# A language-model tower on one core: places of their own for the steps of groups 0, 1, 14, 15 and of the second half's groups 0, 1

## The chip, the cores and the metric

The kernel is one program on one core of a Trainium2 chip. The metric is the device time of one execution in microseconds (us). The kernel before was timed three times: 1875.1, 1875.68 and 1881.88 us, with a median of 1875.68 us. The profile comes from one further execution.

## What is computed

The input is 32 rows of 256 tokens. The reference, cut to what matters:

```python
h = tok_ref(x, ...)                       # embed, 2 layers, head: (32, 256, 256)
#   per layer: LN, q/k/v, causal convolution of k and v by 8 filters, gates,
#   gated linear attention (prefix sums), unit norm, wo, residual,
#   LN, gelu MLP 128-512-128, residual; at the end LN and head 128-256
h = h + attn_ref(_layernorm(h), W_q, W_k, W_v, W_o)   # linear attention, 16 heads of 64, not causal
h = h + ffn_ref(_layernorm(h), w_gate, w_up, w_down)  # silu(gate) * up, 256-768-256
return h
```

## The kernel before

The 32 batch rows are taken two at a time, so there are 16 groups of 512 tokens. The **tower** (function `token_tower`) runs every group through embedding, two layers and the head and stores 512 KB for it in `h_rows`. Its buffers exist four times (streams, group g uses stream g modulo 4). The **second half** (`attention_and_mlp`) loads these rows group by group on two streams, forms the linear attention and the gated MLP, and sends the result. Products of the large matrices are made of three fp32r matmuls (high by high, high by low, low by high), so nearly every input is split by ScalarE (the `high` steps) and VectorE (the `low` steps).

**The order of the work** is written out in tables. A step is a piece of a group's work on one engine: for example `turn` (four transposes on TensorE, L873), `high` (ScalarE, L764) and `low` (VectorE, L619) after it, `av` (TensorE, L972), `chain` (twelve small VectorE instructions ending at L706, a reciprocal square root by Newton steps), `unit` (TensorE, L1000), `mask` (VectorE, L679), `gated` (VectorE, L648 to L659), `q_out` (ScalarE, L773 and L775), `vT_out` (ScalarE, L788), `f1` (TensorE, L820 to L822), `f2` (L1028). In the second half there are `b_load` (a 512 KB load issued by SyncE, L1230), `b_stats` (VectorE, L1275), `rows_high` (GpSimd), `rows_low` (VectorE, L1302), `gram`, `t1`, `keys`, `r`, `m`, `attn` (TensorE), `b_turn` (TensorE, L1440), `b_gate`, `b_up`, `down` (TensorE).

`PLACES_A` and `PLACES_B` hold one place per step for the tower and the second half, `STARTS_A` and `STARTS_B` one start per group; `PREPARE` and `START_UP` hold the preparation of the weights. All steps are sorted by place plus start:

```python
steps = [(at + start, (step, g % STREAMS, l, j, g // STREAMS))
         for g, start in enumerate(STARTS_A) for step, l, j, at in PLACES_A]
...
steps.sort(key=lambda step: step[0])
order = [step for at, step in steps]
```

Each engine then walks this one list and issues the steps that are its own (L1549 to L1579), so that the list fixes the program order of every engine, SyncE's DMA issues included. It fixes the rotation of the PSUM banks too (`uses.add` along the list). Semaphores carry all dependences, so a step whose input is late holds up everything behind it on its engine.

The regions of the four streams are used again by the second half: its V and K weights lie in stream 0's, its rows of group 0 in stream 1's (`b_load` waits for the stores of tower groups 12 and 13), W_q's halves in stream 2's (after group 14's store), its rows of group 1 in stream 3's (after group 15's store). `m_high` waits for group 15's store, and `silu` for all four. `first(s, l, t)` (L462) marks the steps that also wait for the loads and preparations of the start.

Of the kernel before, what the change touches and what calls it, by code (L numbers as in the profile page):

```python
# [35 lines left out]
PLACES_A = [("embed", 0, 0, 832), ("stats", 0, 0, 904), ("pow", 0, 0, 975), ("shift", 0, 0, 944), ("xn", 0, 0, 980),  # L36
            ("turn", 0, 0, 952), ("high", 0, 0, 981), ("low", 0, 0, 974), ("bias", 0, 0, 1928), ("q", 0, 0, 1408),
            ("q_out", 0, 0, 1610), ("kv", 0, 0, 958), ("kv_out", 0, 0, 976), ("kv", 0, 1, 967),
            ("kv_out", 0, 1, 978), ("conv", 0, 0, 974), ("conv_out", 0, 0, 1374), ("conv", 0, 1, 977),
            ("conv_out", 0, 1, 1407), ("turn_v", 0, 0, 1411), ("vT_out", 0, 0, 1610), ("gate", 0, 0, 1650),  # L40
            ("gate_mul", 0, 0, 1791), ("gated", 0, 0, 1838), ("state", 0, 0, 1825), ("state_low", 0, 0, 1893),
            ("floor", 0, 0, 1915), ("qk", 0, 0, 1630), ("mask", 0, 0, 1731), ("qk", 0, 1, 1755),
            ("mask", 0, 1, 1854), ("av", 0, 0, 1815), ("av", 0, 1, 1839), ("av", 0, 2, 1856), ("av", 0, 3, 1877),
            ("apply", 0, 0, 1899), ("norm", 0, 0, 1920), ("sum", 0, 0, 1923), ("chain", 0, 0, 1959),
            ("unit", 0, 0, 1953), ("unit_out", 0, 0, 1974), ("wo", 0, 0, 1959), ("wo_out", 0, 0, 1977),
            ("stats", 1, 0, 1977), ("pow", 1, 0, 2283), ("shift", 1, 0, 1985), ("xn", 1, 0, 2074),
            ("turn", 1, 0, 1982), ("high", 1, 0, 2577), ("low", 1, 0, 2214), ("bias", 1, 0, 2724),
# [3 lines left out]
            ("pow", 2, 0, 2948), ("shift", 2, 0, 2921), ("xn", 2, 0, 2976), ("turn", 2, 0, 2935),  # L51
            ("high", 2, 0, 2981), ("low", 2, 0, 2966), ("bias", 2, 0, 3790), ("q", 1, 0, 2951),
            ("q_out", 1, 0, 2985), ("kv", 1, 0, 2943), ("kv_out", 1, 0, 2971), ("kv", 1, 1, 2946),
            ("kv_out", 1, 1, 2975), ("conv", 1, 0, 2958), ("conv_out", 1, 0, 2986), ("conv", 1, 1, 2960),
            ("conv_out", 1, 1, 2988), ("turn_v", 1, 0, 2967), ("vT_out", 1, 0, 2992), ("gate", 1, 0, 2973),
            ("gate_mul", 1, 0, 2984), ("gated", 1, 0, 2988), ("state", 1, 0, 2984), ("state_low", 1, 0, 2989),
            ("floor", 1, 0, 3579), ("qk", 1, 0, 2975), ("mask", 1, 0, 2984), ("qk", 1, 1, 2982),
            ("mask", 1, 1, 2988), ("av", 1, 0, 2983), ("av", 1, 1, 2985), ("av", 1, 2, 2986), ("av", 1, 3, 2989),
            ("apply", 1, 0, 2991), ("norm", 1, 0, 3599), ("sum", 1, 0, 2998), ("chain", 1, 0, 3282),
            ("unit", 1, 0, 3519), ("unit_out", 1, 0, 3640), ("wo", 1, 0, 3644), ("wo_out", 1, 0, 3791),  # L60
            ("stats", 3, 0, 3797), ("pow", 3, 0, 3942), ("shift", 3, 0, 3845), ("xn", 3, 0, 3823),
            ("turn", 3, 0, 3837), ("high", 3, 0, 3838), ("low", 3, 0, 3883), ("bias", 3, 0, 3947),
# [3 lines left out]
            ("pow", 4, 0, 3999), ("shift", 4, 0, 3979), ("xn", 4, 0, 3995), ("turn", 4, 0, 3981),  # L66
            ("high", 4, 0, 3999), ("low", 4, 0, 3995), ("head", 0, 0, 3994), ("head_out", 0, 0, 3995),
            ("head", 0, 1, 3995), ("head_out", 0, 1, 3996), ("idx", 0, 0, 2611), ("gather", 0, 0, 3031),
            ("gather", 0, 1, 3362), ("gather", 0, 2, 3429), ("gather", 0, 3, 3936), ("store", 0, 0, 3985)]
# [1 line left out]
PLACES_B = [("b_load", 0, 0, 102), ("b_stats", 0, 0, 667), ("b_pow", 0, 0, 838), ("b_xn", 0, 0, 859),
            ("b_turn", 0, 0, 1140), ("b_high", 0, 0, 1170), ("b_low", 0, 0, 1170), ("b_turn", 0, 1, 1159),
            ("b_high", 0, 1, 1224), ("b_low", 0, 1, 1182), ("rows_high", 0, 0, 991), ("rows_low", 0, 0, 906),
            ("gram", 0, 0, 930), ("gram_high", 0, 0, 905), ("gram_low", 0, 0, 930), ("gram", 1, 0, 962),
            ("gram_high", 1, 0, 1003), ("gram_low", 1, 0, 999), ("t1", 0, 0, 975), ("t1_even", 0, 0, 1055),
            ("t1_odd", 0, 0, 994), ("t1", 0, 1, 984), ("t1_even", 0, 1, 1075), ("t1_odd", 0, 1, 999),
            ("keys", 0, 0, 1025), ("keys_out", 0, 0, 1113), ("keys", 0, 1, 1075), ("keys_out", 0, 1, 1125),
            ("r", 0, 0, 1076), ("r_high", 0, 0, 1126), ("r_low", 0, 0, 1104), ("r", 0, 1, 1089),
            ("r_high", 0, 1, 1141), ("r_low", 0, 1, 1123), ("m", 0, 0, 1124), ("m", 0, 1, 1125), ("m", 0, 2, 1126),
            ("m_high", 0, 0, 1169), ("m_low", 0, 0, 1169), ("attn", 0, 0, 1181), ("attn_out", 0, 0, 1189),  # L80
            ("t1", 1, 0, 1000), ("t1_even", 1, 0, 1114), ("t1_odd", 1, 0, 1057), ("t1", 1, 1, 1112),
            ("t1_even", 1, 1, 1169), ("t1_odd", 1, 1, 1168), ("keys", 1, 0, 1142), ("keys_out", 1, 0, 1172),
            ("keys", 1, 1, 1145), ("keys_out", 1, 1, 1202), ("r", 1, 0, 1152), ("r_high", 1, 0, 1220),
            ("r_low", 1, 0, 1172), ("r", 1, 1, 1156), ("r_high", 1, 1, 1221), ("r_low", 1, 1, 1177),
            ("m", 1, 0, 1174), ("m", 1, 1, 1175), ("m", 1, 2, 1176), ("m_high", 1, 0, 1231), ("m_low", 1, 0, 1188),
            ("attn", 1, 0, 1182), ("attn_out", 1, 0, 1197), ("b_stats", 1, 0, 1197), ("b_pow", 1, 0, 1205),
            ("b_xn", 1, 0, 1219), ("b_turn", 1, 0, 1225), ("b_high", 1, 0, 1777), ("b_low", 1, 0, 1227),
            ("b_turn", 1, 1, 1230), ("b_high", 1, 1, 1859), ("b_low", 1, 1, 1231), ("b_gate", 0, 0, 1558),
            ("b_up", 0, 0, 1781), ("silu", 0, 0, 1900), ("hid", 0, 0, 1869), ("hid_high", 0, 0, 1979),
            ("hid_low", 0, 0, 1423), ("b_gate", 1, 0, 1778), ("b_up", 1, 0, 1834), ("silu", 1, 0, 1995),  # L90
            ("hid", 1, 0, 2074), ("hid_high", 1, 0, 2156), ("hid_low", 1, 0, 2326), ("b_gate", 2, 0, 1794),
            ("b_up", 2, 0, 1865), ("silu", 2, 0, 2003), ("hid", 2, 0, 2114), ("hid_high", 2, 0, 2493),
            ("hid_low", 2, 0, 2387), ("b_gate", 3, 0, 1913), ("b_up", 3, 0, 1961), ("silu", 3, 0, 2036),
            ("hid", 3, 0, 2220), ("hid_high", 3, 0, 2494), ("hid_low", 3, 0, 2423), ("b_gate", 4, 0, 1946),
            ("b_up", 4, 0, 2453), ("silu", 4, 0, 2117), ("hid", 4, 0, 2462), ("hid_high", 4, 0, 2496),
            ("hid_low", 4, 0, 2496), ("b_gate", 5, 0, 1970), ("b_up", 5, 0, 2467), ("silu", 5, 0, 2260),
            ("hid", 5, 0, 2468), ("hid_high", 5, 0, 2497), ("hid_low", 5, 0, 2499), ("down", 0, 0, 2422),
            ("down", 1, 0, 2445), ("down", 2, 0, 2467), ("down", 3, 0, 2471), ("down", 4, 0, 2495),
            ("down", 5, 0, 2499), ("add", 0, 0, 2497), ("add", 1, 0, 2498), ("send", 0, 0, 2183)]
# [1541 lines left out]
```

## Time and profile before

| | |
|---|---|
| median of 3 runs | 1875.68 us (1875.1 to 1881.88) |
| profiled execution | 1885.79 us, of which the span is 1883.7 us |
| TensorE matmuls busy | 1806.8 us (96% of the span) |
| VectorE busy | 1099.6 us (58%) |
| ScalarE, GpSimd busy | 726.2 us (39%), 424.4 us (23%) |
| granted TensorE clock, mean | 0.983 |

The tower takes about the first 850 us, the second half the rest; they overlap for some tens of microseconds. "Idle before" is the time that an engine stood still before an instruction, with what released it. A granted clock of 1.00 is 2.4 GHz, one of 0.50 is 1.2 GHz.

### The profile page before, as it was taken

To read this page: it belongs to the slowest core of one execution; us is meant where nothing else is said; L and a number is where in the kernel's file an instruction comes from. 1 tells how busy PE (TensorE), PEld (TensorE's weight loads), DVE (VectorE), ACT (ScalarE), POOL (GpSimd) and SP (SyncE) were. 2 spreads that over 40 slices of the span, in tenths; PEclk is the share of its full clock that TensorE was granted. 3 is DMA by queue.
4 is the path that set the end of the run, shared out by engine and by line. 5 is a ranking of instruction groups with operands and counts; after the bars stand their busy time and mean duration, and the time that the engine had idled before them with its cause. 6 is when DMAs were issued, how large, how long until landed. Compare 5 with 4: busy or idle time off the path is not lost.

```text
span 1883.7 us, 41798 instructions
## 1 busy us (share of the span) xinstructions
PE 1806.8 (96%) x17146; PEld 1583.0 (84%) x17146; DVE 1099.6 (58%) x2955; ACT 726.2 (39%) x1508; POOL 424.4 (23%) x391
## 2 busy tenths in 40 slices
PE   5899999999999999868999999999999999999998
PEld 4788888888888888657888888988888888888887
DVE  3688888888888887555444445444444444444443
ACT  2455555555555555423323232233233322323232
POOL 4233333333333322110122102210211121122102
PEclk9899999999999999878999999999999999999999
DMA  3000000000000001012000000000000000000000
GB/s 97 8 7 18 19 18 19 19 18 18 19 18 18 28 13 69 12 45 74 1 23 23 11 14 23 24 1 23 23 24 2 23 23 24 2 23 23 1 23 23
DMA packets 29355, 42.39 MB, mean 23 GB/s; under 512 B 6000, under 2 KB 22768, under 8 KB 29168
## 3 DMA queue, kind: packets, MB, share of 16 engines
q1 hardware_dynamic: 26160, 35.07, 5.7%
q0 software_dynamic: 2048, 4.20, 0.9%
q8 instruction: 138, 2.26, 0.5%
q10 hardware_dynamic: 960, 0.46, 0.1%
q14 instruction: 49, 0.40, 0.1%
HBM read 22.93 MB, written 16.78 MB: 21 GB/s over the span
## 4 chain that ended last, share of the span: by engine, by line
PE 80%; DVE 11%; issue 4%; DMA 2%; POOL 1%; ACT 1%; SPq 0%; DVEq 0%; POOLq 0%; ACTq 0%
PE ps L1426 14%; PE ps L1427 13%; PE ps L1428 13%; PE ps L1028 5%; PE ps L1476 3%; PE ps L972 3%; PE ps L1492 3%; PE ps L956 3%; PE ps L905 2%; PE ps L820 2%; DMA h<-h_rows 2%; PE ps L822 2%; PE ps L821 2%; PE ps L873 2%; PE ps L1440 2%
## 5 line engine op out<-in xcount | busy, mean ns | idle before, releaser
L1265 POOL TENSOR_TENSOR hids_low<-hid,hids_high 128x512 fp32r<-128x512 f32 x96 | 125.6, 1309 | 773.9 <-ACT hids_high L1412 773.9
L521 POOL TENSOR_TENSOR rstd<-var,minus_half 128x4 f32<-128x4 f32 x80 | 81.7, 1021 | 453.6 <-DVE var L608 453.6
L679 DVE TENSOR_TENSOR att<-ps,causal 128x512 f32<-128x512 f32 x256 | 158.8, 684 | 18.4 <-PE ps L956 17.1
L759 ACT ACTIVATE xn<-x,shift,rstd 128x128 f32<-128x128 f32 x320 | 131.3, 486 | 90.6 <-DVE shift L613 90.6
L1426 PE MATMUL ps<-r_high,wq_high 128*128 128x256 f32 x512 | 144.9, 283 | 0.6 <-issue 0.6
L1428 PE MATMUL ps<-r_high,wq_low 128*128 128x256 f32 x512 | 144.9, 283 | 0.0
L1427 PE MATMUL ps<-r_low,wq_high 128*128 128x256 f32 x512 | 144.9, 283 | 0.0
L1028 PE MATMUL ps<-w_f,wide 128*128 128x128 f32 x1024 | 127.1, 278 | 0.0
L1412 ACT ACTIVATE hids_high<-hid 128x512 fp32r<-128x512 f32 x96 | 60.4, 629 | 169.6 <-PE ps L1428 124.7
L1328 DVE TENSOR_TENSOR m_low<-ps,m_high 128x512 fp32r<-128x512 f32 x32 | 22.1, 691 | 176.8 <-ACT m_high L1398 176.8
L1028 PEld LDWEIGHTS ps<-w_f,wide 128*128 128x128 f32 x1024 | 119.4, 192 | 5.2 <-issue 5.0
L1322 DVE TENSOR_TENSOR r_low<-ps,r_high 128x512 fp32r<-128x512 f32 x128 | 79.5, 684 | 60.6 <-ACT r_high L1390 60.6
L1426 PE MATMUL ps<-wd_high,hids_high 128*128 128x256 f32 x384 | 111.4, 290 | 0.7 <-POOL hids_low L1265 0.7
L1406 ACT ACTIVATE silu<-ps 128x512 f32<-128x512 f32 x96 | 55.5, 594 | 141.2 <-PE ps L1428 106.6
L815 ACT ACTIVATE wide<-ps,b_f 128x512 f32<-128x512 f32 x128 | 83.1, 697 | 68.6 <-PE ps L822 68.5
L1314 DVE COPY t<-ps 128x512 f32<-128x512 f32 x64 | 44.3, 692 | 111.1 <-PE ps L1428 62.8
L1428 PE MATMUL ps<-wd_high,hids_low 128*128 128x256 f32 x384 | 108.7, 283 | 0.0
L1427 PE MATMUL ps<-wd_low,hids_high 128*128 128x256 f32 x384 | 108.5, 283 | 0.0
L1341 DVE TENSOR_TENSOR hid<-silu,ps 128x512 f32<-128x512 f32 x96 | 65.0, 683 | 66.4 <-PE ps L1428 54.1
L1426 PE MATMUL ps<-wv_high,gram_high 128*128 128x512 f32 x256 | 103.3, 404 | 0.0
L1398 ACT ACTIVATE m_high<-ps 128x512 fp32r<-128x512 f32 x32 | 19.1, 597 | 211.9 <-PE ps L1428 198.9
L1427 PE MATMUL ps<-wv_low,gram_high 128*128 128x512 f32 x256 | 99.8, 390 | 0.0
(350 smaller groups left out, 5042.2 us busy)
## 6 DMA issues: line engine op xcount, KB each, us to landing
h_rows<-h_out SPq DMA_DIRECT2D x16, 512.0 KB, 2.7
h<-h_rows SPq DMA_DIRECT2D x16, 512.0 KB, 3.9
out<-bxn SPq DMA_DIRECT2D x32, 256.0 KB, 2.3
emb<-in_embed,idx POOLq DMA_INDIRECT x64, 2.6
taps<-in_filters SPq DMA_DIRECT2D x1, 1024.0 KB, 5.7
stage<-in_W_vT SPq DMA_DIRECT2D x2, 512.0 KB, 5.7
wk<-in_W_kT SPq DMA_DIRECT2D x1, 1024.0 KB, 5.0
wo<-in_W_oT SPq DMA_DIRECT2D x1, 1024.0 KB, 9.4
```

Source lines behind the costliest of these rows:

```text
L521: pool.tensor_tensor(rstd[s][:], var[s][:], minus_half[:], ALU.pow)\
L679: dve.tensor_tensor(masked[:, :, PAIR * g:PAIR * g + PAIR, :], bank("qk", s, l, j, g, t)[:].rearrange("p (n r t) -> p n r t", n=2, r=PAIR) ...
L759: act.activation(xn[s][:, j, :], x[s][:, j, :], ACT.Identity, bias=shift[s][:, j:j + 1], scale=rstd[s][:, j:j + 1]).then_inc(xn_made[s].se ...
L815: act.activation(gl[s][:, j, :], bank("f1", s, l, j, t)[:], ACT.Gelu_apprx_tanh, bias=b_f1[:, l, j:j + 1]).then_inc(gl_made[s].sem, 1)
L1028: ins = pe.matmul(out[:, D * j:D * j + D], gl[s][:, f, P * j:P * j + P], w_f2[l][:, f, :], start=(f == 0 and j == 0), stop=(f == FC - 1), ...
L1265: pool.tensor_tensor(hids[1][:, halves, :], hid[:, half, :], hids[0][:, halves, :].bitcast(F32), ALU.subtract).then_inc(hid_low[s].sem, 1)
L1322: dve.tensor_tensor(low, bank("r", s, b, k, t)[:], high.bitcast(F32), ALU.subtract)\
L1341: dve.tensor_tensor(hid[:, uses.place["hid", s, b, t], :], silu[:, uses.place["silu", s, b, t], :], bank("b_up", s, b, t)[:], ALU.mult).th ...
L1412: act.activation(hids[0][:, uses.place["hids", s, b, t], :], hid[:, uses.place["hid", s, b, t], :], ACT.Copy).then_inc(hid_high[s].sem, 1)
L1426: pe.matmul(out, lhsT[0], rhs[0], start=start, stop=False, **kw)
L1427: pe.matmul(out, lhsT[0], rhs[1], start=False, stop=False, **kw)
L1428: return pe.matmul(out, lhsT[1], rhs[0], start=False, stop=stop, **kw)
```

## The change

No instruction that computes is added or removed. Four edits:

1. All places and starts of the common tables are multiplied by ten, which leaves their order as it was.
2. `MOVED_A` gives steps of tower groups 0, 1, 14 and 15 places of their own, `MOVED_B` steps of the second half's groups 0 and 1.
3. `PREPARE` and `START_UP` have new places. Steps of equal place from `START_UP` now come ahead of the tower's.
4. `first` holds for the first turn of all four streams, not of stream 0 alone, so the waits for loads and preparations are issued for groups 1, 2 and 3 too.

```diff
-STARTS_A = [547, 1549, 2550, 3551, 4553, 5555, 6557, 7559, 8560, 9562, 10563, 11565, 12567, 13569, 14570, 15572]
+STARTS_A = [5470, 15490, 25500, 35510, 45530, 55550, 65570, 75590, 85600, 95620, 105630, 115650, 125670, 135690,
+            145700, 155720]
+MOVED_A = [(0, "stats", 0, 0, -76025), (0, "shift", 0, 0, -76005), (0, "xn", 0, 0, 13137), (0, "turn", 0, 0, -45339),
...
+           (0, "kv_out", 0, 1, -75070), (0, "turn_v", 0, 0, 14315), (0, "vT_out", 0, 0, 15282),
...
+           (1, "shift", 0, 0, -85089), (1, "xn", 0, 0, 5589), (1, "turn", 0, 0, 8871), (1, "high", 0, 0, 5590),
...
+           (15, "turn", 3, 0, 29891), (15, "high", 3, 0, 37621), (15, "low", 3, 0, 36528), (15, "bias", 3, 0, 39502),
...
+MOVED_B = [(0, "b_load", 0, 0, -7399), (0, "b_stats", 0, 0, -108), (0, "b_pow", 0, 0, 984), (0, "b_xn", 0, 0, 796),
...
+           (0, "rows_high", 0, 0, 8680), (0, "rows_low", 0, 0, 5152), (0, "gram", 0, 0, 10),
...
+           (1, "b_load", 0, 0, -1393), (1, "b_stats", 0, 0, -5523), (1, "b_pow", 0, 0, -758),
...
+           (1, "rows_high", 0, 0, -459), (1, "rows_low", 0, 0, -5068), (1, "gram", 0, 0, -2327),
...
-    steps = [(at + start, (step, g % STREAMS, l, j, g // STREAMS))
+    moved = {(g, step, l, j): at for g, step, l, j, at in MOVED_A}
+    steps = [(moved.get((g, step, l, j), at) + start, (step, g % STREAMS, l, j, g // STREAMS))
              for g, start in enumerate(STARTS_A) for step, l, j, at in PLACES_A]
...
-    steps += [(at, (step, n, 0, 0, 0)) for step, n, at in START_UP]
+    steps[:0] = [(at, (step, n, 0, 0, 0)) for step, n, at in START_UP]
 
     def first(s, l, t):
-        return s == l == t == 0
+        return l == t == 0
...
-        steps += [(at + start, (step, g % B_STREAMS, b, n, g // B_STREAMS))
+        moved = {(g, step, b, n): at for g, step, b, n, at in MOVED_B}
+        steps += [(moved.get((g, step, b, n), at) + start, (step, g % B_STREAMS, b, n, g // B_STREAMS))
                   for g, start in enumerate(STARTS_B) for step, b, n, at in PLACES_B]
```

Sorting the two sets of tables by hand gives what changes for each engine. Of TensorE's 1652 steps the order differs in 270, all of them among the first 182 and among numbers 758 to 1028. Orders that matter below, of the kernel after:

| where | before | after |
|---|---|---|
| start, ScalarE | `q_out`, `vT_out` of group 0 | `vT_out`, `q_out` |
| start, VectorE | group 0: `mask`, `gate_mul`, `gated`, `mask` | `gate_mul`, `gated`, `mask`, `mask` |
| start, TensorE | group 0: `sum`, `unit`; group 1: `turn`; then `wo`, `kv`, `kv`, `conv`; `q` later | group 1 `turn`, `sum`, `f1_bias`, group 1 `kv`, `q`, then `unit`, `kv`, `wo`, `conv` |
| start, GpSimd | gathers of groups 1 and 2, then `embed` of group 1 | gathers of group 1, its `embed` and `pow`, then gathers of 2 and 3 |
| end of tower, TensorE | ..., `av` 0 and later steps of 15, both `head` of 14, `sum` 15, `unit` 15, `wo` 15, `turn` 15, three `f1` 15, `gram` of the second half's group 0 | `sum` 15, `unit` 15, `wo` 15, `gram`, `head` 14, `turn` 15, `head` 14, four `f1` 15 |
| end of tower, SyncE | store 14, then `b_load` 0 | store 13, `b_load` 0, then store 14 |
| end of tower, SyncE | store 15, `w_load` 4, 5, `b_load` 1, `w_load` 6 | `w_load` 4, 5, store 15, `w_load` 6, `b_load` 1 |
| end of tower, VectorE | group 15's `unit_out`, `b_stats` 0, `wo_out` | `b_stats` 0 ahead of 14's `f2_out` and 15's `gate_mul`; `unit_out`, `rows_low` 0, `wo_out` |
| second half, TensorE | `attn` 0, `attn` 0, `b_turn` 0, `b_turn` 0, `b_gate` 0 ... then `gram` of group 1 | a `gram` of group 1 amid `m` 0; `attn`, `attn`, `gram`, `t1`, `t1` of group 1, then `b_turn`, `b_turn`, `keys`, `keys`, `t1` of 1, `b_gate` 0 |

## Rows read from the trace of the kernel before

**Rows 1.** The page: span and busy time of TensorE.

```profile
span 1883.7 us, 41798 instructions
...
PE 1806.8 (96%) x17146; PEld 1583.0 (84%) x17146; DVE 1099.6 (58%) x2955; ACT 726.2 (39%) x1508; POOL 424.4 (23%) x391
```

**Rows 2.** Windows: length, busy time (and instructions) of each engine, clock, DMA share, GB/s.

```profile
0.00:47.00 47.00, 27.42 (x221) 21.98 (x221) 18.54 (x66) 11.27 (x26) 19.85 (x26) 0.93 0.38 98
47.00:94.00 47.00, 38.43 (x347) 33.40 (x348) 28.44 (x88) 19.94 (x43) 12.14 (x12) 0.82 0.03 8
...
376.00:470.00 94.00, 93.49 (x1055) 82.00 (x1053) 77.69 (x250) 50.81 (x115) 30.98 (x30) 1.00 0.06 18
...
752.00:800.00 48.00, 39.94 (x348) 33.06 (x349) 28.21 (x81) 21.12 (x45) 9.06 (x8) 0.89 0.03 12
800.00:848.00 48.00, 33.87 (x236) 28.46 (x237) 27.00 (x74) 13.28 (x25) 5.32 (x5) 0.79 0.14 44
848.00:896.00 48.00, 40.47 (x389) 34.94 (x388) 25.72 (x54) 17.43 (x30) 3.02 (x3) 0.89 0.22 72
```

**Rows 3.** Timeline of TensorE, the start: start, length, instruction, [idle before, releaser].

```profile
49.29 1.11 PE L1000 MATMUL ps<-ident,sq 128*128 128x128 f32 x4 [3.12 <-DVE sq L706]
...
57.08 3.27 PE L905 MATMUL ps<-wide,taps 128*128 128x128 f32 x16 [1.86 <-DVE wide L627]
...
83.92 0.58 PE L820 MATMUL ps<-w_kv1h,xT0h 128*128 128x256 f32 x1 [2.67 <-DVE xT0l L619]
```

**Rows 4.** Timeline of ScalarE and VectorE in the start, group 0's first layer.

```profile
29.02 1.45 ACT L773 ACTIVATE wide<-ps,b_q_part,parity 128x512 f32<-128x512 f32 x2 [0.22 <-PE ps L822]
...
30.72 0.60 ACT L788 ACTIVATE vT<-ps 128x512 f32<-128x512 f32 x1
...
32.62 2.48 DVE L679 TENSOR_TENSOR att<-ps,causal 128x512 f32<-128x512 f32 x4 [7.99 <-PE ps L956]
```

**Rows 5.** Timeline of TensorE, the end of the tower.

```profile
758.23 1.08 PE L972 MATMUL ps<-att,gk 128*32 128x128 f32 x16 [2.63 <-DVE gk L659]
...
780.90 0.50 PE L820 MATMUL ps<-xT2h,w_f11h 128*128 128x512 f32 x1 [1.48 <-DVE xT2l L619]
...
803.84 0.64 PE L972 MATMUL ps<-att,gk 128*32 128x128 f32 x16 [2.56 <-DVE gk L659]
...
814.44 0.66 PE L1000 MATMUL ps<-ident,sq 128*128 128x128 f32 x4 [3.11 <-DVE sq L706]
815.94 2.07 PE L1008 MATMUL ps<-w_o,h_out 128*128 128x128 f32 x8 [0.85 <-DVE h_out L713]
823.36 1.54 PE L873 MATMUL ps<-ident,xn 128*128 128x128 f32 x4 [5.34 <-ACT xn L759]
```

**Rows 6.** Timeline of TensorE, the second half's group 0.

```profile
882.48 1.97 PE L1440 MATMUL ps<-ident,bxn 128*128 128x128 f32 x8 [5.45 <-DVE bxn L1291]
885.86 0.80 PE L1426 MATMUL ps<-bxT_high,wg_high 128*128 128x512 f32 x1 [1.41 <-DVE bxT_low L1297]
```

**Rows 7.** Windows around the gaps of the change-over, columns as in rows 2.

```profile
814.40:832.50 18.10, 10.39 (x35) 8.19 (x36) 8.03 (x27) 5.04 (x8) 4.30 (x4) 0.53 0.24 77
...
877.00:890.50 13.50, 6.64 (x20) 5.24 (x20) 8.61 (x20) 3.25 (x5) 1.01 (x1) 0.62 0.21 58
```

**Rows 8.** Window of the second half's group 1: `gram` and two `t1`.

```profile
903.21:910.39 7.18, 7.16 (x38) 6.01 (x37) 2.62 (x5) 2.85 (x5) 0.00 (x0) 1.00 0.01 2
```

**Rows 9.** Timelines of VectorE and SyncE: `b_stats` and the loads of both groups.

```profile
816.95 1.40 DVE L1275 BATCH_NORM_STATS2 bstats<-h 128x6 f32<-128x256 f32 x4 [1.07 <-DMA h<-h_rows]
...
893.06 1.39 DVE L1275 BATCH_NORM_STATS2 bstats<-h 128x6 f32<-128x256 f32 x4
...
853.49 0.33 SPq L1230 DMA_DIRECT2D h<-h_rows  x1
```

**Rows 10.** The page's DMA issues: KB each, us to landing.

```profile
h_rows<-h_out SPq DMA_DIRECT2D x16, 512.0 KB, 2.7
h<-h_rows SPq DMA_DIRECT2D x16, 512.0 KB, 3.9
```

More of the change, by code:

```diff
@@ L33 @@
 GK_SLOTS, ATT_SLOTS = 1, 2
[L36 to L47, printed above, removed]
[3 rows of a table removed]
[L51 to L62, printed above, removed]
[3 rows of a table removed]
[L66 to L69, printed above, removed]
@@ L70 @@
-STARTS_A = [547, 1549, 2550, 3551, 4553, 5555, 6557, 7559, 8560, 9562, 10563, 11565, 12567, 13569, 14570, 15572]
[L71 to L99, printed above, removed]
@@ L112 @@
[L112 to L118 removed]
+PLACES_A = [("embed", 0, 0, 8320), ("stats", 0, 0, 9040), ("pow", 0, 0, 9750), ("shift", 0, 0, 9440),
+            ("xn", 0, 0, 9800), ("turn", 0, 0, 9520), ("high", 0, 0, 9810), ("low", 0, 0, 9740),
+            ("bias", 0, 0, 19280), ("q", 0, 0, 14080), ("q_out", 0, 0, 16100), ("kv", 0, 0, 9580),
+            ("kv_out", 0, 0, 9760), ("kv", 0, 1, 9670), ("kv_out", 0, 1, 9780), ("conv", 0, 0, 9740),
+            ("conv_out", 0, 0, 13740), ("conv", 0, 1, 9770), ("conv_out", 0, 1, 14070), ("turn_v", 0, 0, 14110),
+            ("vT_out", 0, 0, 16100), ("gate", 0, 0, 16500), ("gate_mul", 0, 0, 17910), ("gated", 0, 0, 18380),
+            ("state", 0, 0, 18250), ("state_low", 0, 0, 18930), ("floor", 0, 0, 19150), ("qk", 0, 0, 16300),
+            ("mask", 0, 0, 17310), ("qk", 0, 1, 17550), ("mask", 0, 1, 18540), ("av", 0, 0, 18150),
+            ("av", 0, 1, 18390), ("av", 0, 2, 18560), ("av", 0, 3, 18770), ("apply", 0, 0, 18990),
+            ("norm", 0, 0, 19200), ("sum", 0, 0, 19230), ("chain", 0, 0, 19590), ("unit", 0, 0, 19530),
+            ("unit_out", 0, 0, 19740), ("wo", 0, 0, 19590), ("wo_out", 0, 0, 19770), ("stats", 1, 0, 19770),
+            ("pow", 1, 0, 22830), ("shift", 1, 0, 19850), ("xn", 1, 0, 20740), ("turn", 1, 0, 19820),
+            ("high", 1, 0, 25770), ("low", 1, 0, 22140), ("bias", 1, 0, 27240), ("f1", 0, 0, 24270),
[3 rows of a table added]
+            ("stats", 2, 0, 28980), ("pow", 2, 0, 29480), ("shift", 2, 0, 29210), ("xn", 2, 0, 29760),
+            ("turn", 2, 0, 29350), ("high", 2, 0, 29810), ("low", 2, 0, 29660), ("bias", 2, 0, 37900),
+            ("q", 1, 0, 29510), ("q_out", 1, 0, 29850), ("kv", 1, 0, 29430), ("kv_out", 1, 0, 29710),
+            ("kv", 1, 1, 29460), ("kv_out", 1, 1, 29750), ("conv", 1, 0, 29580), ("conv_out", 1, 0, 29860),
+            ("conv", 1, 1, 29600), ("conv_out", 1, 1, 29880), ("turn_v", 1, 0, 29670), ("vT_out", 1, 0, 29920),
+            ("gate", 1, 0, 29730), ("gate_mul", 1, 0, 29840), ("gated", 1, 0, 29880), ("state", 1, 0, 29840),
+            ("state_low", 1, 0, 29890), ("floor", 1, 0, 35790), ("qk", 1, 0, 29750), ("mask", 1, 0, 29840),
+            ("qk", 1, 1, 29820), ("mask", 1, 1, 29880), ("av", 1, 0, 29830), ("av", 1, 1, 29850),
+            ("av", 1, 2, 29860), ("av", 1, 3, 29890), ("apply", 1, 0, 29910), ("norm", 1, 0, 35990),
+            ("sum", 1, 0, 29980), ("chain", 1, 0, 32820), ("unit", 1, 0, 35190), ("unit_out", 1, 0, 36400),
+            ("wo", 1, 0, 36440), ("wo_out", 1, 0, 37910), ("stats", 3, 0, 37970), ("pow", 3, 0, 39420),
+            ("shift", 3, 0, 38450), ("xn", 3, 0, 38230), ("turn", 3, 0, 38370), ("high", 3, 0, 38380),
+            ("low", 3, 0, 38830), ("bias", 3, 0, 39470), ("f1", 1, 0, 38940), ("gelu", 1, 0, 38770),
[3 rows of a table added]
+            ("pow", 4, 0, 39990), ("shift", 4, 0, 39790), ("xn", 4, 0, 39950), ("turn", 4, 0, 39810),
+            ("high", 4, 0, 39990), ("low", 4, 0, 39950), ("head", 0, 0, 39940), ("head_out", 0, 0, 39950),
+            ("head", 0, 1, 39950), ("head_out", 0, 1, 39960), ("idx", 0, 0, 26110), ("gather", 0, 0, 30310),
+            ("gather", 0, 1, 33620), ("gather", 0, 2, 34290), ("gather", 0, 3, 39360), ("store", 0, 0, 39850)]
```

235 lines of the change are left out of this document (216 added, 19 removed), and 42 rows, old and new, of tables (MOVED_A, MOVED_B, PLACES_A).

## The prediction

> **What bounds the kernel now.** The page's busy times come first: TensorE is at work for 1806.8 of 1883.7 us, no other engine for more than 58% [rows 1]. So TensorE's program order decides, and only about 77 us are its idle time. The windows say where these lie: the first 94 us lack 28 us of matmul work (47.00 less 27.42, plus 47.00 less 38.43), the 144 us from 752 to 896 lack 29.7, a steady stretch of 94 us only 0.5 [rows 2]. The same stretches have a mean granted clock of 0.79 to 0.93 where the steady one has 1.00, so some of their matmuls run at 1.2 GHz for 2.4. These are the only stretches whose order the change touches. I then read TensorE's timeline there for what ends each gap [rows 3, 5, 6], and the timelines of the other engines for how their own order delays it [rows 4, 9].
>
> The profiled execution took 1885.79 us, 10.1 above the median of 1875.68. I sum against the profile and take the difference from the median. A measurement of this kernel can tell some 0.5% (9.4 us) from no change: its three runs span 0.4%.
>
> **The start.** The first matmuls wait for the embedding of group 0, which does not come sooner. The first gain is in its first layer. ScalarE now makes `vT_out` (0.60 us) ahead of `q_out` (1.45 plus a third activation, 1.8 in all) [rows 4], so `gate` runs 2 us sooner, `gate_mul` and `gated` go ahead of the first `mask` (2.48 us), and `av`, which waits for `gated` and the first `mask`, can start 1.1 us sooner. The larger part is what stands around `unit`, which waits 3.12 us for `chain`, and around `conv`, which waits 1.86 us for group 1's `kv_out` [rows 3]. After the change `f1_bias`, a `kv` and `q` of group 1 lie between `sum` and `unit`, as that group's embedding no longer stands behind group 2's gathers on GpSimd. These 3 to 4.5 us of matmul work fill the 3.12 us, and `conv` starts at about 54 for 57.08 with `q` (0.9 us) already done: 4 us for the start up to there, the 1.1 included. Bounds are 1 (the `unit` is held back by as much as it hides) and 7 (the two gaps, 5.0, and the low clock around them). The 2.67 us before group 0's second `kv` [rows 3] shrink by `unit` of group 1, now ahead of it (0.7 us), and by 0.7 because the `shift` of group 2 no longer stands before `chain`: 1.4. Start: **5.4**. The extra waits of `first`, some twenty for each of three groups on TensorE, are on semaphores long complete. They cost nothing while matmuls are queued behind one another, as everywhere in the steady stretch; without that cover I bound them at 2 us. GpSimd's gathers for groups 2 and 3 now run back to back, ten microseconds, when its next duty (`bias` of group 0) has 13 us to spare.
>
> **The tower's end, up to group 14's attention and MLP.** Gaps of 2.63 and 1.48 us stand before `av` and `f1` [rows 5]. The new order moves group 15's `turn` into the first, but also a split of W_v (1.22 us of VectorE) in front of the `stats` that lead to it, and a late `head_out` ahead of the `low` that ends the second. Walking both chains, `av` comes some 0.5 us later, with 1.1 us of `turn` behind it, and `f1` 0.9 us later or, if the clock stays up, 2 sooner: **0**, bounds -3 and 3.
>
> **Group 15's last layer.** This serial chain leaves TensorE idle 2.56 us before `av`, 3.11 and 0.85 around `unit`, 5.34 before `turn` [rows 5]. The chain itself shortens. In the kernel before VectorE runs `b_stats` (2.1 us in three instructions from 816.95 on [rows 9]) before `wo_out`, though `wo` had ended at 818.01: 1.0 us. Both `head` steps of group 14 (1.7 us) and their two `head_out` stood before `chain`; now `sum` and `chain` come first and the heads lie in the 5.34 us gap: 1.5 us more. `gated` goes ahead of the first `mask`, 1.2 us. So `f1` comes 3.6 us sooner, with `gram` of the second half's group 0 (2.5 us as it ran) already done in the gap. In the window from 814.4 the clock is 0.53 [rows 7], and the three `f1` run there at 1.2 GHz, 1.5 us each for 0.9; with the gap filled I expect them at full speed, 1.9 us. That would be 8.0; I take **6.9**, since the `low` step now waits for a `head_out` as well. Bounds 3 (heads and `gram` fill, the chain and the clock gain nothing) and 10. The window from 848 on has 7.5 us of idle time [rows 2], of which the next part explains 6.9; for the rest, where `m` is moved about, and a like one just before it at a `t1`, I take **0.8**, bounds 0 and 1.4.
>
> **The second half's group 0.** From 877 on TensorE waits 5.45 us for group 0's residual, statistics, power and normalisation, then 1.41 for a split [rows 6]. After the change `gram`, `t1`, `t1` of group 1 stand there, 7.2 us of work at full clock [rows 8], and more before `b_gate`. The two gaps are 6.9 us. The clock in the window is 0.62 [rows 7]: nearly all of its 6.64 us of matmuls ran at 1.2 GHz and would take about half, 3.3 us. Sum **10.2**. This needs group 1's rows in time. The store of tower group 15 is issued at about 843 by my walk, lands 2.7 us later, `b_load` takes 3.9 [rows 10], `b_stats` 2.1, power 1.0, `b_xn` 1.4, `rows_high` 1.1, `rows_low` 1.2 behind 2.5 us of `r_low`: about 860.5, where TensorE reaches `gram` at 861.5. In the kernel before the load was issued at 853.49 and `b_stats` began at 893.06 only [rows 9], so the place in the order had been the limit, not the data. If it is late by 5 us the term is 5.
>
> **Sum.** 5.4 + 0 + 6.9 + 0.8 + 10.2 = 23.3 us, 1885.8 to 1862.5 in a profiled execution like that one, or 1875.7 to **1852** for the median. All engines' steady order is the same, so nothing is given back there.
>
> One rule speaks against counting the clock. The clock's part of the sum is about 5.2 us (1.9 and 3.3), taken from matmuls that ran at 0.53 and 0.62 and the same ones at 1.00. The Trainium skill, "TensorE: Matmul & The Clock Gate", Part 1, says that the ramp penalty is under 1% of a typical kernel and that one should not fit to a count of slow matmuls; by it the sum would be 18.1 us and the time 1857. I keep the term, as the rows show the same matmul at both lengths.
>
> **Rivals.** *Only the second half gains.* The filled gaps in the tower come back as later ones, as the chain of dependent steps there sets the pace. The rows for it: group 15's gaps are all ended by the chain itself, not by order. Then 10.2 and some 1.5 of the rest stay: 1864. *Group 1 late, or gaps only moved.* VectorE now meets `b_stats` of group 0 before 14's `f2_out` and 15's `gate_mul`, and `b_stats` of group 1 amid group 0's `m`. It stands still until each load lands, and TensorE with it. The first load follows a store that now waits for group 13's second `head_out`, at about 778; 778 + 2.7 + 3.9 is 785, VectorE reaches it at 789. From 4 us of lateness on it costs one for one; both together late by 10 us would leave some 2 to 8 us of gain: 1870. *The clock stays low.* From 757 to 832 TensorE has some 57 us of busy time, of which about 22 ran at 1.2 GHz. If the new order thins the work just enough, the other 35 could run at half rate too: 35 more, less the 23.3: 1887. It decides only if over 23 of these 35 us are hit. Against it: every low stretch in the rows follows gaps, and there are fewer. *The clock stays high* at the start and in the tower's end: 10 us more gain, 1842.
>
> **How the numbers follow.** Forecast 0.55; clock high 0.12; second half alone 0.18; gaps moved 0.11; clock low 0.04. The limit for faster is 1866.3, so the first three give 0.85, the fourth is within 0.5%, the last slower. The low bounds of the terms (1.7, -3, 3, 0, 5) sum to 6.7, or 1869; the high ones (8.4, 3, 10, 1.4, 10.2) to 33, or 1842.7. The range of 1840 to 1868 leaves out most of the last two cases.
>
> **What would show it.** Right: no gap over 1 us between 870 and 890 and a clock of 1.00 there; `f1` of group 15's second layer some 3 us sooner and `gram` before it; `conv` of group 1 at about 54. Wrong: a wait for a landing before either `b_stats` that grows past 2 us, TensorE waiting for `xns_low` before `gram`, or a clock below 0.9 in more windows than before.

## The result and the profile after

| | before | after |
|---|---|---|
| median of 5 executions each | 1875.8 us (1875.1 to 1883.12) | 1865.78 us (1864.04 to 1868.14) |
| ratio of the two, 95% interval | | 0.9934 (0.9914 to 0.9955) |
| profiled execution | 1885.79 us | 1865.78 us |
| TensorE busy / idle within the span | 1806.8 / 76.9 us | 1797.3 / 66.6 us |
| granted clock, mean | 0.983 | 0.992 |

The kernel is faster by 10.0 us, or 0.7% by the ratio. The time lies in the predicted range (1840 to 1868), but 13.8 us above the predicted 1852. The two profiles differ by twice as much, 20.0 us, so a good part of the question is which of the two differences is the change's own.

The page of the kernel after:

```profile
span 1863.9 us, 41852 instructions
...
PE 1797.3 (96%) x17146; PEld 1575.1 (85%) x17146; DVE 1098.1 (59%) x2955; ACT 726.5 (39%) x1508; POOL 426.4 (23%) x391
```

Its windows, cut like those of [rows 2]:

```profile
0.00:47.00 47.00, 24.89 (x207) 20.37 (x207) 18.99 (x60) 11.66 (x27) 23.54 (x30) 0.93 0.40 103
47.00:94.00 47.00, 41.02 (x398) 35.17 (x397) 33.48 (x109) 21.97 (x48) 13.11 (x13) 0.93 0.02 5
376.00:470.00 94.00, 93.49 (x1054) 81.94 (x1053) 77.63 (x251) 50.72 (x114) 30.69 (x31) 1.00 0.06 19
752.00:800.00 48.00, 39.16 (x393) 32.58 (x395) 32.38 (x97) 19.36 (x41) 7.51 (x7) 0.96 0.06 23
800.00:848.00 48.00, 40.69 (x352) 34.80 (x341) 27.02 (x63) 18.70 (x36) 6.39 (x5) 0.89 0.22 74
848.00:896.00 48.00, 47.44 (x481) 40.81 (x483) 29.38 (x60) 19.71 (x36) 6.60 (x5) 1.00 0.07 22
```

The steady stretch is as before. In the window from 848 TensorE does 47.44 us of work for 40.47 at a clock of 1.00 for 0.89; in the one from 800, 40.69 for 33.87. At the start the busy time is the same, 65.91 us of 94 for 65.85, but the clock of the second window is 0.93 for 0.82, and the counts are 207 and 398 matmuls for 221 and 347: 37 more in the same busy time.

TensorE's timeline at the start, to be read beside [rows 3]:

```profile
37.25 0.64 PE L1182 MATMUL ps<-att,gk 128*32 128x128 f32 x16 [2.82 <-DVE att L889]
...
39.89 0.41 PE L1153 MATMUL ps<-gate,ones 128*128 128x16 f32 x2 [0.93 <-issue]
...
42.55 0.87 PE L1182 MATMUL ps<-att,gk 128*32 128x128 f32 x12 [1.23 <-DVE att L889]
...
51.86 0.84 PE L1210 MATMUL ps<-ident,sq 128*128 128x128 f32 x4
...
54.56 1.95 PE L1115 MATMUL ps<-wide,taps 128*128 128x128 f32 x16
...
78.08 1.39 PE L1083 MATMUL ps<-ident,xn 128*128 128x128 f32 x4 [1.52 <-ACT xn L969]
```

`unit` (L1210) has no wait where it had 3.12 us, and `conv` (L1115) begins at 54.56 instead of 57.08, without its wait. But four waits stand here that were shorter or absent in the kernel before: 2.82 and 1.23 us for the masks (`av` had one wait of 0.92, as `mask` then came before `gate_mul`), 0.93 with no releaser, and 1.52 for a `turn`, which had 0.45.

The end of the tower, beside [rows 5]:

```profile
776.33 0.79 PE L1030 MATMUL ps<-xT2h,w_f11h 128*128 128x512 f32 x1 [1.48 <-DVE xT2l L829]
...
797.23 1.08 PE L1182 MATMUL ps<-att,gk 128*32 128x128 f32 x32 [2.44 <-DVE att L889]
802.13 1.06 PE L1202 MATMUL ps<-same_head,sq 128*128 128x8 f32 x8 [0.69 <-ACT sq L1017]
807.16 1.12 PE L1210 MATMUL ps<-ident,sq 128*128 128x128 f32 x4 [3.97 <-DVE sq L916]
809.12 2.08 PE L1218 MATMUL ps<-w_o,h_out 128*128 128x128 f32 x8 [0.85 <-DVE h_out L923]
815.89 1.54 PE L1083 MATMUL ps<-ident,xn 128*128 128x128 f32 x4 [1.49 <-ACT xn L969]
```

The gap before `turn` fell from 5.34 to 1.49 us, the one before `unit` grew from 3.11 to 3.97: the same chain of VectorE's, with less work of others beside it. Next the second half, where 5.45 and 1.41 us were idle [rows 6] at a clock of 0.62 [rows 7]: the window in which TensorE now passes that place, and the two rows on which the prediction made it hang, SyncE's load of group 1 and VectorE's `b_stats` on it:

```profile
867.00:881.50 14.50, 14.50 (x129) 12.42 (x128) 10.81 (x24) 5.14 (x9) 1.38 (x1) 1.00 0.01 1
```

```profile
843.91 0.33 SPq L1441 DMA_DIRECT2D h<-h_rows  x1
```

```profile
848.62 1.41 DVE L1486 BATCH_NORM_STATS2 bstats<-h 128x6 f32<-128x256 f32 x4 [2.62 <-DMA h<-h_rows]
```

No idle time, full clock. `b_stats` waits 2.62 us for the landing. The prediction named a wait of over 2 us there as a sign of being wrong; it came, but cost TensorE nothing: VectorE had the time to spare, and `gram` runs at 857.85, 3.6 us ahead of the walk in the prediction.

### The profile page after: what moved, and what is told of

Its sections match the earlier page's. It is cut to its first block, busy times and chain, and to the rows that moved or that the text cites. A ratio compares the mean times of both kernels' runs of the same rounds, so it can differ in the third digit from the quotient of the medians.

```text
span 1863.9 us, 41852 instructions
## 1 busy us (share of the span) xinstructions
PE 1797.3 (96%) x17146; PEld 1575.1 (85%) x17146; DVE 1098.1 (59%) x2955; ACT 726.5 (39%) x1508; POOL 426.4 (23%) x391
## 4 chain that ended last, share of the span: by engine, by line
PE 79%; DVE 12%; issue 3%; DMA 3%; POOL 2%; ACT 1%; SPq 0%; another core or an unknown queue 0%; DVEq 0%; POOLq 0%; ACTq 0%
PE ps L1637 14%; PE ps L1638 13%; PE ps L1639 13%; PE ps L1238 5%; PE ps L1687 3%; PE ps L1182 3%; PE ps L1703 3%; PE ps L1030 3%; PE ps L1166 3%; PE ps L1115 2%; PE ps L1032 2%; PE ps L1031 2%; DMA h<-h_rows 2%; DVE att L889 2%; PE ps L1083 2%
## 5 line engine op out<-in xcount | busy, mean ns | idle before, releaser
L1639 PE MATMUL ps<-wv_high,gram_low 128*128 128x512 f32 x256 | 99.8, 390 | 0.0
```

Of the source, the lines that this page charges most:

```text
L1639: return pe.matmul(out, lhsT[1], rhs[0], start=False, stop=stop, **kw)
```

## The experiments

Twelve kernels in three comparisons, each with its own executions of the kernel before (medians 1880.13 of 29, 1880.42 of 11, 1880.03 of 17). Medians, numbers of executions and ratios:

| kernel | median, us | ratio to before (95%) |
|---|---|---|
| 1st: w_waits | 1883.44 (12) | 1.0017 (1.0005 to 1.0029) |
| 1st: s_start | 1882.85 (12) | 1.0018 (1.0007 to 1.0028) |
| 1st: tb_end | 1868.44 (6) | 0.9944 (0.9932 to 0.9956) |
| 1st: n_nofill | 1875.75 (12) | 0.9984 (0.9975 to 0.9992) |
| 2nd: after_again | 1863.39 (6) | 0.9906 (0.9885 to 0.9927) |
| 2nd: old_first | 1859.43 (6) | 0.9894 (0.9874 to 0.9914) |
| 2nd: send_late | 1854.83 (5) | 0.9870 (0.9850 to 0.9890) |
| 2nd: heads_back | 1861.21 (6) | 0.9898 (0.9879 to 0.9918) |
| 3rd: start_2 | 1883.21 (12) | 1.0015 (1.0002 to 1.0028) |
| 3rd: end_2 | 1867.62 (5) | 0.9937 (0.9924 to 0.9950) |
| 3rd: after_3 | 1869.96 (6) | 0.9949 (0.9937 to 0.9962) |
| 3rd: best | 1854.72 (4) | 0.9875 (0.9859 to 0.9891) |

The same table from the profiles, one execution each. TensorE's time is cut at three steps whose work before them is the same in all: the first `turn` of tower group 4, that of group 14, and `gram` of the second half's group 2. Length / idle time in it, in us:

| profile | up to group 4 | group 4 to 14 | the change-over | to the end |
|---|---|---|---|---|
| before | 182.3 / 29.9 | 470.1 / 3.0 | 314.7 / 31.2 | 911.8 / 8.0 |
| w_waits | 181.7 / 30.9 | 470.7 / 3.4 | 310.8 / 30.4 | 912.1 / 7.7 |
| s_start | 183.5 / 29.1 | 470.4 / 3.2 | 310.9 / 30.9 | 912.2 / 8.2 |
| start_2 | 183.1 / 29.3 | 470.4 / 3.2 | 311.7 / 30.1 | 912.4 / 8.4 |
| tb_end | 184.8 / 30.4 | 470.2 / 3.4 | 297.1 / 20.4 | 913.0 / 8.0 |
| end_2 | 182.5 / 29.8 | 470.0 / 3.3 | 295.9 / 20.8 | 912.4 / 7.5 |
| after | 179.0 / 29.6 | 470.1 / 3.2 | 295.1 / 19.8 | 914.7 / 8.9 |
| after_again | 175.9 / 27.8 | 469.9 / 3.1 | 296.1 / 19.4 | 913.7 / 8.6 |
| after_3 | 182.2 / 29.1 | 469.9 / 3.2 | 299.9 / 17.8 | 911.7 / 6.8 |
| n_nofill | 179.2 / 29.1 | 469.9 / 3.2 | 304.4 / 26.7 | 913.1 / 8.1 |
| heads_back | 173.7 / 27.8 | 469.9 / 3.1 | 299.9 / 21.5 | 909.9 / 5.7 |
| old_first | 176.7 / 26.8 | 469.6 / 2.8 | 295.5 / 19.2 | 908.2 / 4.1 |
| send_late | 174.9 / 27.3 | 469.8 / 3.1 | 297.8 / 19.8 | 903.5 / 0.7 |
| best | 177.3 / 28.8 | 469.6 / 2.8 | 296.4 / 20.0 | 903.6 / 0.7 |

Each cut lies at the end of the `turn`, or within the `gram`. Between kernels of one order the idle time of the first three parts repeats within 3 us; in the last it ranges from 4.1 to 8.9 us among the kernels with `send` in its old place. Busy time (length less idle) repeats less well: up to group 4 it is 146.0 to 154.4 us for the same matmuls in the same order (the ten with the new start). That goes with the clock: in after_again (148.1 us) the mean granted clock of that part is 0.97, in after_3 (153.1 us) 0.94.

### w_waits: the extra waits alone

```diff
-MOVED_A = [(0, "stats", 0, 0, -76025), ...
-MOVED_B = [(0, "b_load", 0, 0, -7399), ...
+MOVED_A = []
+MOVED_B = []
```
`PREPARE` and `START_UP` have their old places, times ten.

> The order of the kernel before on every engine, with only the changed rule for the extra waits of the first turn (fourth edit): the waits alone. Theory 'waits are free' (they stand on semaphores long complete): the time of the kernel before, 1875.8 us, within 1. Rival 'they cost up to the 2 us bound of the prediction': 1877 to 1878, with the start later by 2 us in the profile. As the order is that of before, this run also gives a second profiled execution of it: by the theory that the profiled execution of before was an unlucky one (10 us over its median, from more time at the low clock), this profile has fewer low stretches than the nine counted in that of before, and its span less its time at the low clock is the same; by the rival that the profiler or a wait adds the 10 us, the profile is again at about 1885 with the same stretches.

1883.44 us, 3.3 above the kernel before: above the bound of 2, and neither theory. The profile doesn't show them: 72.4 us of idle time in the four parts for 72.1. It is shorter than the profile of before by 3.6 us, all of it busy time (150.7 for 152.4 up to group 4, 280.4 for 283.5 at the change-over). Its profiled execution took 1882.16 us, no more than the others of its series, so profiling itself adds nothing that shows, and that of before was a long one.

### s_start and start_2: the start alone

```diff
+MOVED_A = [m for m in MOVED_A if m[0] in (0, 1)]
+MOVED_B = []
```
(written out as tables), `PREPARE` old.

> The start's part alone: the new places of groups 0 and 1 and of the start-up, the extra waits; tower end, preparation and second half in the old order. Theory 'the start's gain is kept through the tower' (the trace after the change is 3.2 us ahead in the steady tower): 1875.8 - 3.2 = 1872.6, and in the profile the first steps of group 5 some 3 us sooner. Rival 'the full 5.4 forecast, of which a late start-up step at the second layer of group 0 costs 2 only together with the rest': 1870.4. Rival 'it is lost again at the tower's end, where chains and not TensorE's order decide': 1875.8, with the lead gone by the end of group 15.

> The start's part alone (as s_start), in a second load and in one comparison with the end's part and the whole. Theory 'the start is worth what the profiles show': over the ten profiles so far the fifth tower group begins at 177.7 us on the mean with the new start (seven) and at 182.9 with the old one (three), of which 3.3 are idle time; 1880.3 - 5 = 1875.3, and this profile has less than 20 us of low clock before 110 us. Rival 'with the old end behind it, it gives nothing', as first measured (1882.9 beside 1883.4 with the old start and the same waits): 1880 to 1883 again, with some 27 us of low clock before 110 us. The program is the same there as in the whole, so by this rival something is fixed by the load or the code's place and not by the order.

1882.85 and 1883.21 us: not faster than the waits alone, twice. Up to group 4 the idle time is 29.1 and 29.3 us for 29.9 before: what the filled gaps gave has come back as others. The busy time is 154.4 and 153.8 for 152.4. The clock of the windows of start_2 and of after_again, which have the same order there:

```profile
0.00:58.00 58.00, 35.95 (x259) 30.78 (x260) 25.73 (x82) 13.83 (x31) 23.48 (x30) 0.85 0.32 84
58.00:95.00 37.00, 31.29 (x313) 26.55 (x313) 25.31 (x84) 16.75 (x38) 12.07 (x13) 0.91 0.01 3
```

```profile
0.00:58.00 58.00, 35.58 (x320) 29.59 (x320) 29.43 (x96) 18.89 (x43) 26.56 (x33) 0.97 0.32 84
58.00:95.00 37.00, 33.09 (x352) 28.66 (x351) 27.31 (x83) 15.86 (x35) 11.63 (x12) 0.91 0.02 5
```

TensorE is busy for 36 of the first 58 us in both; at a clock of 0.85 it gets 259 matmuls done, at 0.97 320. after_3, the whole change, fell like start_2 (0.85). So the clock of the start isn't the order's doing alone. The first expectation's 1872.6 and the second's 1875.3 are refuted; the second one's rival, 1880 to 1883 with much low clock again, came about.

### tb_end and end_2: the end alone

```diff
+MOVED_A = [m for m in MOVED_A if m[0] in (14, 15)]
```
`START_UP` old; `MOVED_B` and `PREPARE` as after the change.

> The end's part alone: new places of groups 14 and 15, of the preparation and of the second half's groups 0 and 1; the start in the old order (only the extra waits are left there). Theory 'the parts add, the start being worth 3.2': 1865.8 + 3.2 = 1869.0. Rival 'the start's gain is lost at the tower's end': 1865.8. Rival 'nearly all of the 10 us between the medians is the start' : 1873 or more.

> The end's part alone (as tb_end), second load. By its first timing 1868.4, that is 12 us less than the 1880.3 of the kernel before, extra waits included. Theory 'parts add': this and the start's part sum to the whole's 16 us: 1868 to 1869. Rival 'the load decides by 3 us and more': a median outside 1865 to 1872.

1868.44 and 1867.62 us: 12 us below the kernel before, 15.4 below the waits alone. The change-over is 14.9 and 16.1 us shorter than the mean of the four profiles with the old order there (312.0). This part holds nearly all of the gain.

### after_again and after_3: the whole change again

> The kernel after, unchanged, timed once more beside many executions of the one before, as the medians of three and five runs differ from those of 29 (1880.13 for the kernel before). Theory 'the two medians first shown were low draws of the kernel before': 1866 again, a mean gain of 14 us, of which some 10 are less time at the low clock. Rival 'the gain is the 10 us of the first comparison': 1870 here. The profile: the start runs at the low clock for 14 us, as in the two profiles with this start and the new end, or for 27, as in the profile of the start alone; if 27, the clock's share of the start is chance and not the order's doing.

> The whole change, third load. Medians so far 1865.8 and 1863.4, executions from 1857.5 to 1868.1. Theory 'the kernel before is at 1880.3 and the gain 16 us': 1864. Rival 'the first comparison': 1870 less than 5 us away from the end's part alone.

1863.39 and 1869.96 us: the one lies below its theory's 1866, the other on its rival's 1870. With the first comparison the gain is 10.0, 17.0 and 10.1 us, with intervals of the second and third that don't meet. Over all 17 executions of the one (mean 1866.2) and 62 of the other (mean 1879.8) it is **13.6 us**, 0.7%. after_3 has the least idle time of the three and is the slowest: 17.8 us at the change-over, but 282.1 of busy time there for 275.3 and 276.7, at a mean granted clock of 0.95 for 0.98 and 0.97.

### n_nofill: group 1's work put behind the gap again

```diff
-           (0, "b_turn", 1, 0, 13713), (0, "b_turn", 1, 1, 13714),
+           (0, "b_turn", 1, 0, 13552), (0, "b_turn", 1, 1, 13552),
...
-           (1, "gram_high", 1, 0, -1806), (1, "gram_low", 1, 0, -2498),
+           (1, "gram_high", 1, 0, -1802), (1, "gram_low", 1, 0, -650),
```
and in the same way `t1_even` and `t1_odd` 0 and 1 of group 1, and its `keys_out` 0.

> The kernel after, with one part undone: the two b_turn of the second half's group 0 come again straight after its attn, ahead of gram, t1, t1 of group 1 (with the splits of these moved behind those of b_turn on ScalarE and VectorE). The steps of group 1 are all still ahead of b_gate. Theory 'the fill is worth its gap and the clock behind it': the gap of 5.45 us before b_turn is back, the clock falls once, 1865.8 + 5.5 + 3 = 1874.3. Theory 'the gap alone': 1871.3. Rival 'group 1's rows are there early, so what TensorE does in that gap is only drawn from the order behind it, and another wait takes its place': 1867 or less, with the gap in the profile and as much less idle time behind it.

1875.75 us, about 9 above the whole change (1866.2 to 1867.1 over its 17 executions). The gap and the clock around it are back, in TensorE's timeline and in a window:

```profile
873.97 0.47 PE L1646 MATMUL ps<-ident,bxn 128*128 128x128 f32 x1 [5.83 <-DVE bxn L1497]
```

```profile
868.00:884.00 16.00, 10.17 (x48) 8.81 (x48) 9.29 (x21) 4.04 (x6) 1.37 (x1) 0.79 0.00 0
```

The change-over is 7.7 us longer than the mean of the eight that have the new end whole (296.7), 7.1 of it idle time (26.7 for 19.7). Of these 7.1, 5.83 are the gap; an earlier `b_turn` waits 1.64 us for 0.52 in the kernel after. 'Gap and clock' (1874.3) is the theory that comes nearest, and no other wait took the gap's place.

### heads_back: both heads of group 14 ahead of the chain again

```diff
-           (14, "head_out", 0, 0, 46547), (14, "head_out", 0, 1, 46549)
+           (14, "head_out", 0, 0, 45052), (14, "head_out", 0, 1, 45052)
...
-           (15, "sum", 1, 0, 29890), (15, "unit", 1, 0, 29890), (15, "wo", 1, 0, 29890),
+           (15, "sum", 1, 0, 29891), (15, "unit", 1, 0, 29891), (15, "wo", 1, 0, 29891),
```
with `turn`, `f1` 0 and `gram` of the second half's group 0 kept behind them.

> The kernel after with both head steps of group 14 put back ahead of sum of group 15 on TensorE, and both head_out ahead of its chain on VectorE, as they stood before. The prediction counted their move at 1.5 us of a shorter chain. Theory 'the chain sets the end of the tower': the chain starts 1.0 (sum behind the heads, whose 1.6 us meet a gap of 0.7) + 1.4 (two head_out) later, and the heads no longer fill the gaps behind wo: f1 of group 15's second layer some 2.5 us later, 1868.4. Rival 'the heads fill the 3.97 us that TensorE waits before unit, so they cost only VectorE's part': 1867.2. Rival 'the slack is drawn from the second half's work': 1866.

1861.21 us beside 1863.39: the executions (1856.9 to 1864.5 and 1857.5 to 1867.1) can't tell 2 us. The timeline can. heads_back, then after_again:

```profile
793.02 1.93 PE L1171 MATMUL ps<-att,gk 128*32 128x128 f32 x32 [2.44 <-DVE att L878]
...
805.79 0.66 PE L1199 MATMUL ps<-ident,sq 128*128 128x128 f32 x4 [3.12 <-DVE sq L905]
...
814.12 1.54 PE L1072 MATMUL ps<-ident,xn 128*128 128x128 f32 x4 [2.19 <-ACT xn L958]
817.14 0.80 PE L1019 MATMUL ps<-xT3h,w_f11h 128*128 128x512 f32 x1 [1.48 <-DVE xT3l L818]
```

```profile
795.23 1.93 PE L1182 MATMUL ps<-att,gk 128*32 128x128 f32 x32 [2.42 <-DVE att L889]
...
806.56 1.12 PE L1210 MATMUL ps<-ident,sq 128*128 128x128 f32 x4 [3.85 <-DVE sq L916]
...
815.02 1.39 PE L1083 MATMUL ps<-ident,xn 128*128 128x128 f32 x4 [1.52 <-ACT xn L969]
817.89 0.50 PE L1030 MATMUL ps<-xT3h,w_f11h 128*128 128x512 f32 x1 [0.77 <-DVE xT3l L829]
```

From `av` to `f1` it is 24.12 us with the heads in front and 22.66 without: 1.5 us, with a gap before `unit` of 3.12 for 3.85. That is near what the first rival gave for VectorE's part (1.4) and below the theory's 2.5. It is one profile of each.

### old_first: the whole change without the extra waits

```diff
-        return l == t == 0
+        return s == l == t == 0
```

> The kernel after with the old rule for the extra waits of the first turn (group 0 alone), all places as in the kernel after. Theory 'the waits cost 2.5 us', from 1883.4 of the waits alone beside 1880.1 of the kernel before: 1863. Rival 'they stand behind queued matmuls and cost nothing, and the 3 us are a difference between two loads of one program': 1866.

1859.43 us, 4.0 below after_again and below both theories; the executions of the two overlap (1856.2 to 1864.5 and 1857.5 to 1867.1). Of the 6.0 us less idle time in its profile 1.4 lie before tower group 14 and 4.5 before `gram` of the second half's later groups, where no wait was changed. What these are, the next experiment and the last section show.

### send_late and best: one place in the common table

```diff
-            ("add", 1, 0, 24980), ("send", 0, 0, 21830)]
+            ("add", 1, 0, 24980), ("send", 0, 0, 26500)]
```
best has the old `first` too.

> The kernel after with one place of the common table changed: send comes behind the load of the group after next on SyncE, in every group and not in group 0 alone. In the profile of the kernel after, TensorE waits before gram of seven groups for a chain that begins with this load, 8.0 us in all, and the load is issued 1.0 us after send's two issues begin. Theory 'the chain moves with the load': each of these gaps shrinks by up to 1.0, in all 6 us: 1860. Rival 'the send now lands later and b_xn, which waits for it, takes the load's place': 1866 or more. Rival 'the rows wait on GpSimd and VectorE in turn, so the later engine decides': 2 us or less.

> The kernel after with send behind the load of the group after next and with the old rule for the extra waits. Theory 'both add' (8.6 us by medians for the first, 4.0 for the second, of which some of the second was the same gaps before gram): 1854.8 less 1 to 2 us for the idle time of the first four groups: 1853. Rival 'the waits cost nothing, their 4 us were the gaps before gram alone, which send's place has closed already': 1855. In the profile: no gap before gram of any group, idle time of TensorE under 50 us.

1854.83 us, 8.6 below after_again and 5 below the theory's 1860, and 1854.72: **faster than both kernels, by 1.3% of the one before.** The gaps before `gram` are gone: 0.7 us idle in the whole last part, for 8.6. Leaving out the waits gives nothing here: best lies on its rival's 1855, but four executions from 1853.8 to 1859.2 can't exclude the 1853 of 'both add'. Its idle time is 52.3 us where under 50 was expected. The kernel after, group 4, in SyncE's, VectorE's, GpSimd's and TensorE's timelines:

```profile
1059.22 0.89 SPq L1461 DMA_DIRECT2D out<-bxn  x2
1060.22 0.42 SPq L1441 DMA_DIRECT2D h<-h_rows  x1
```

```profile
1064.75 1.41 DVE L1486 BATCH_NORM_STATS2 bstats<-h 128x6 f32<-128x256 f32 x4 [2.12 <-DMA h<-h_rows]
...
1070.68 2.29 DVE L1513 TENSOR_TENSOR xns_low<-bxn,xns_high 128x1024 fp32r<-128x1024 f32 x1 [1.28 <-POOL xns_high L1471]
```

```profile
1070.62 1.28 POOL L1476 TENSOR_TENSOR hids_low<-hid,hids_high 128x512 fp32r<-128x512 f32 x1
```

```profile
1073.03 0.38 PE L1637 MATMUL ps<-xns_high 128*128 128x256 f32 x1 [1.60 <-DVE xns_low L1513]
```

and send_late:

```profile
1057.34 0.34 SPq L1440 DMA_DIRECT2D h<-h_rows  x1
1057.79 0.88 SPq L1460 DMA_DIRECT2D out<-bxn  x2
```

```profile
1061.39 1.41 DVE L1485 BATCH_NORM_STATS2 bstats<-h 128x6 f32<-128x256 f32 x4 [0.62 <-DMA h<-h_rows]
...
1067.43 1.23 DVE L1512 TENSOR_TENSOR xns_low<-bxn,xns_high 128x1024 fp32r<-128x1024 f32 x1 [1.29 <-POOL xns_high L1470]
```

```profile
1068.08 1.72 POOL L1475 TENSOR_TENSOR hids_low<-hid,hids_high 128x512 fp32r<-128x512 f32 x1 [0.69 <-ACT hids_high L1622]
```

VectorE's wait for the load falls from 2.12 to 0.62 us, as the load stands first. And `xns_low` takes 1.23 us for 2.29: now it, and not GpSimd's `hids_low`, starts first.

## Why the prediction was right and where it failed

**The second half's group 0** (10.2): right. Undoing the fill of its first gap alone costs 7.7 us by the profile and about 9 by the medians; the second gap of 1.4 stays filled in that run. The walk to group 1's rows held: store at 840.68 for 843, `gram` at 857.85 for 861.5. Its terms add up to 858.9 for `xns_low`, not to the 860.5 that it gives; in the profile after that step ended at 856.90.

**Group 15's last layer** (6.9) and the small gaps (0.8): `f1` begins 7.46 us sooner (818.92 for 826.38), of which 4.57 are the lead that group 14's `f1` had already (776.33 for 780.90): 2.9 for the 3.6 named, with `gram` done. The heads' share is 1.5 as worked out. The three `f1` did not all run at full speed: in the first a matmul takes 0.63 us still and from the second on 0.39, and `gram` itself ran mostly at 0.41 where 0.28 is full speed. The whole change-over gives 15.3 us on the mean of four and eight profiles, for 17.9 predicted: 11.0 less idle time (30.6 to 19.7) and 4.3 less busy time, with the mean granted clock there at 0.93 to 0.95 in the four and 0.95 to 0.98 in the others. That less the fill's two gaps (7.7 and 1.4) leaves 6.2 for 7.7. Which of the steps taken out of the chain gave the rest beside the heads, `b_stats` or `gated` ahead of `mask`, no run here separates.

**The tower's end to group 14** (0): about 1 us better in the first pair of profiles, within the bounds.

**The start** (5.4): wrong in its mechanism. The gaps before `unit` and `conv` (3.12, 1.86) are gone as foretold, and so is that before the second `kv` (2.67, foretold to shrink by 1.4), with 0.85 left before `unit` of group 1. But up to group 4 TensorE is idle for 29.6 us in the profile after, for 29.9 before, and for 28.5 and 30.3 on the means of ten and four profiles: the waits for masks and `turn` took most of their place. The step that failed costed `gate_mul` ahead of `mask` as a gain of 1.1 for `av`; `av` came 0.6 sooner (37.25 for 37.88) and its second part then waited 1.23 us for the other mask, and nothing was booked for the `turn` behind it. Of the 3.3 us by which the profile after leads at group 4, 3.0 are busy time (149.4 for 152.4), the clock's, and that is chance in part. Timed, the start gave 0.6 and 0.2 us over the waits alone. Over the end alone it gave 1.8 by the medians of two series and the mean of all executions (1868.0 to 1866.2), but in the one comparison that has both, the end alone was 2.3 us faster than the whole (1867.62 and 1869.96). So the timings can't tell the start's gain from nothing.

**The extra waits** (0, bound 2): the three series with the waits and the old end lie at 1882.9 to 1883.4, some 3 us above the kernel before, and no profile shows them as idle time; best, without them, is no faster than send_late, with them. This stays open.

**The sum.** Timed, the parts are 15.4 for the end (1883.4 to 1868.0), 1.8 for the start (not told from nothing, as said), 3.3 lost with the waits: 13.9 beside the 13.6 of the whole. The prediction had 17.9, 5.4 and 0. So 2.5, 3.6 and 3.3 us are the three misses of the gain, 9.4 of the 13.8. The other 4.4 are the base: "I sum against the profile and take the difference from the median". The three executions shown, with a median of 1875.68, lay that much low among 62 (1873.8 to 1886.8, median 1880.06). The profiled one lay high, with a clock of 0.983 where 29 have 0.985 on the mean, by an estimate from these some 3 to 4 us of matmul time. That is part of why the first pair of profiles shows 20.0 us. That the time still fell inside the range owes something to luck: the later series of the same kernel have medians of 1863.39 and 1869.96, and the last is outside it.

**The clock's term** (5.2) was weighed against a rule. In the traces the busy time of the change-over fell by 4.3 us on the mean, as the term says; but for the whole, idle time fell by 12.9 (72.1 to 59.1, mean of three profiles) and the timed gain is 13.6. The Trainium skill, "TensorE: Matmul & The Clock Gate", Part 1, says not to fit a kernel's cost to a count of slow matmuls; by it the time would have been 1857, closer, and the 146.0 to 154.4 us of busy time for one order speak for it: what the clock gives varies by more than the term.

The rivals: 'only the second half gains' named 1864, nearer the 1865.78 measured than the forecast's 1852, but by a mechanism that occurred only at the start: the 6.2 us of the change-over beside the fill are mostly the tower's. 'Clock high' occurred in some starts, 'clock low' in after_3, by some 6 us of its change-over and not by 35.
